# A message product in three rounded products, every second message unsplit, in the edge stage of a graph network kernel

## What is computed

```python
h = jnp.maximum(_layernorm(x, axis=-1), 0.0)
m_in = jnp.concatenate([h[src], edge_attr], axis=1)      # 512 + 128 features
m = jax.nn.relu(m_in @ W1.T + b1) @ W2.T + b2
agg = jax.ops.segment_sum(m, dst, num_segments=h.shape[0])
```

## Time and profile before

| | us |
|---|---|
| median of 3 runs | 1405.14 (1401.69 to 1405.39) |
| the profiled execution | 1408.71 |
| its span, first to last instruction | 1407.0 |
| cell stage, 292 to 527 | 235 |
| P stage, 757 to 808 | 51 |
| edge stage, 808 to 1116 | 308 |
| TensorE / VectorE / GpSimd / ScalarE busy over the span | 1260.4 / 1015.7 / 713.9 / 582.9 |

### The profile page before, as it was taken

One profiled execution on the slowest core, in us unless ns is written; L12 is line 12 of the kernel. 1 busy time (PEld: TensorE's weight loads), 2 busy tenths in 40 slices (PEclk: granted clock), 3 DMA queues, 4 the chain that ended last, 5 costly groups with the idle time before them and its releaser, 6 DMA issues.

```text
span 1407.0 us, 20310 instructions
## 1 busy us (share of the span) xinstructions
PE 1260.4 (90%) x4504; PEld 753.1 (54%) x4504; DVE 1015.7 (72%) x1944; ACT 582.9 (41%) x1470; POOL 713.9 (51%) x873
## 2 busy tenths in 40 slices
PE   4764989949898889899997889999999899998998
PEld 2532444423333335457875644445445488886787
DVE  9568625359899889752368568889898799888543
ACT  0210221146666650212011178888888743334210
POOL 0577677767787761776667066666667300000000
PEclk9987999979999999999999999999999999999999
DMA  8851252230000008334224477777777300002231
GB/s 331 292 167 31 91 179 67 68 130 25 17 19 17 17 6 312 116 112 136 83 83 136 161 225 215 223 230 225 222 221 229 93 0 1 0 1 86 75 94 36
DMA packets 87257, 167.93 MB, mean 119 GB/s; under 512 B 16124, under 2 KB 44670, under 8 KB 84644
## 3 DMA queue, kind: packets, MB, share of 16 engines
q1 hardware_dynamic: 59588, 102.72, 22.0%
q0 software_dynamic: 25472, 59.97, 14.2%
q10 hardware_dynamic: 2144, 4.59, 1.1%
HBM read 115.97 MB, written 51.25 MB: 119 GB/s over the span
## 4 chain that ended last, share of the span: by engine, by line
PE 44%; issue 22%; POOL 15%; DVE 9%; DMA 6%; DVEq 2%; POOLq 1%; ACT 1%; SPq 0%; ACTq 0%
POOL cell_rows L707 9%; PE pb L1231 6%; PE pb L1239 6%; PE pb L1434 5%; POOL arena L818 5%; PE pb L1407 4%; PE pb L1408 4%; PE pb L1409 4%; DMA arena<-p_rows,gidx 4%; DVE arena L1690 2%; PE pb L1339 2%; PE pb L1205 2%; PE pb L1123 2%; DMA cell_rows<-tiles,gidx 2%; PE pb L1311 1%
## 5 line engine op out<-in xcount | busy, mean ns | idle before, releaser
L818 POOL DMA_INDIRECT arena<-p_rows,gidx x184 | 191.6, 1042 | 65.4 <-issue 64.5
L753 POOL DMA_INDIRECT dst_rows<-ering,gidx x168 | 168.6, 1004 | 103.1 <-issue 95.7
L707 POOL DMA_INDIRECT cell_rows<-tiles,gidx x168 | 169.1, 1007 | 68.0 <-issue 53.8
L1339 PE MATMUL pb<-arena 128*128 128x512 f32 x368 | 189.8, 599 | 4.3 <-ACT arena L990 4.3
L1690 DVE TENSOR_TENSOR arena<-pb,arena 128x384 f32 x272 | 151.8, 558 | 26.6 <-PE pb L1205 24.4
L1827 DVE TENSOR_TENSOR arena<-pb,arena 128x512 f32<-128x512 f32 x184 | 124.2, 686 | 39.9 <-DMA arena<-p_rows,gidx 29.7
L881 ACT ACTIVATE arena<-iota,free 128x128 f32<-128x128 f32 x272 | 94.3, 393 | 86.3 <-PE pb L1205 69.7
L1205 PE MATMUL pb<-arena 128*128 128x384 f32 x272 | 105.6, 515 | 19.1 <-POOL arena L760 19.1
L1205 PE MATMUL pb<-tiles,arena 128*128 128x384 f32 x272 | 103.3, 505 | 19.7 <-DVE arena L1690 17.0
L1355 PE MATMUL pb<-high,low 128*128 128x512 f32 x138 | 92.0, 666 | 8.2 <-DVE arena L1842 5.4
L1834 DVE SCALAR_TENSOR_TENSOR low<-arena,high 128x512 fp32r<-128x512 f32 x138 | 94.5, 685 | 3.4 <-issue 0.8
(11 more groups left out here) (307 smaller groups left out, 2539.6 us busy)
## 6 DMA issues: line engine op xcount, KB each, us to landing
dst_rows<-arena SPq DMA_DIRECT2D x6, 2046.0 KB, 17.5
ering<-in_edge_attr_dram SPq DMA_DIRECT2D x41, 256.0 KB
arena<-adj SPq DMA_DIRECT2D x10, 640.0 KB, 4.1
arena<-dst_rows SPq DMA_DIRECT2D x24, 264.0 KB
arena<-wt_gru SPq DMA_DIRECT2D x48, 128.0 KB
ws<-dst_rows SPq DMA_DIRECT2D x22, 264.0 KB
arena<-in_x_dram SPq DMA_DIRECT2D x18, 256.0 KB
arena<-in_L_gnn_W_hh_dram SPq DMA_DIRECT2D x3, 1024.0 KB
```

Source lines behind the costliest of these rows:

```text
L707: nc.gpsimd.indirect_dma_start(cell_rows[:, :], bass.IndirectOffsetOnAxis(gidx[:, SPAN * a + k:SPAN * a + k + 1], 0), cring[:, a, k], None ...
L753: nc.gpsimd.indirect_dma_start(dst_rows[:, :], bass.IndirectOffsetOnAxis(gidx[:, k:k + 1], 0), ering[:, k, :], None).then_inc(e_scattered[ ...
L818: nc.gpsimd.indirect_dma_start(rows[:, k, :], None, p_rows[:, :], bass.IndirectOffsetOnAxis(gidx[:, k:k + 1], 0)).then_inc(g_landed[k], 16)
L1339: nc.tensor.matmul(e_bank(k)[:], erowT[:, k % 4], w1e_sb, start=True, stop=True).then_inc(edge_mm, 1)
```

## The change

In the **edge stage** the attributes are split too. ScalarE copies them rounded (`erowT[:, 0]`), a new VectorE operation `low_row` subtracts that from the bank and writes the rest (`erowT[:, 1]`), and `m_edges` is three rounded products with W1e split in the same way (`w1e_high`, `w1e_low`, made once). Since VectorE now reads the bank as well, `t_edges` and `m_edges` wait for a new semaphore `row_split`, which `low_row` raises. TensorE and ScalarE turn and copy attributes five chunks ahead in place of four; `low_row` runs four ahead. Every second message is summed whole (`SPLIT = 0`), in place of every fourth. GpSimd reads the sources' numbers where they lie in the loaded columns, with no copy to `gidx`; SP's loads therefore wait for `msg_added`, where they waited for `g_ready`.

In the **P stage** tiles 0 and 1 are turned one step of the second layer earlier, and `low_h2` of tiles 0 to 2 is made within that layer. The reciprocal and the products of the batch norm are made behind the last tile of P; the variance is loaded later, to another place. In the **cell stage** VectorE loads 32 addresses at a time (`READ`), in 9 turns for 17.

```diff
-WHOLE = 3
+SPLIT = 0
...
+        erowT = sb_behind(low.shape[1] + 6 * KT * D + GROUP * (D + EW), "erowT", [P, 2, 4, P], F32R)
...
+        READ = 4 * TURN
...
-                    at_least(sp, g_ready, WIDE // 4 * i + q - 3)
+                    at_least(sp, msg_added, WIDE * i + 4 * q - 12)
...
-            def index_quarter(i, q):
...
-                nc.gpsimd.tensor_copy(gidx[:, k:k + 4], edge_rows(4 * q, 4).bitcast(I32)[:, :, DE]).then_inc(g_ready, 1)
...
+                    nc.gpsimd.indirect_dma_start(rows[:, k % GROUP, :], None, p_rows[:, :],
+                                                 bass.IndirectOffsetOnAxis(edge_rows(k).bitcast(I32)[:, 0, DE:DE + 1], 0)
+                                                 ).then_inc(g_landed[k % GROUP], 16)
...
-                nc.scalar.copy(erowT[:, k % 4], pb[k % 2][:, 0:P]).then_inc(turned_read, 1)
+                nc.scalar.copy(erowT[:, 0, k % 4], pb[k % 2][:, 0:P]).then_inc(turned_read, 1)
...
-                    if not last or k + 4 < n:
-                        turned_copy(c + 4, k + 4)
+                    if not last or k + 5 < n:
+                        turned_copy(c + 5, k + 5)
...
-                at_least(pe, turned_read, c - 1)
+                at_least(pe, row_split, c - 1)
                 nc.tensor.transpose(pb[k % 2][:, 0:P], edge_rows(k)[:, 0, 0:DE], ident[:]).then_inc(turned, 1)
...
-                pe.wait_ge(turned_read, c + 1)
+                pe.wait_ge(row_split, c + 1)
                 at_least(pe, msg_added, c - 3)
-                nc.tensor.matmul(e_bank(k)[:], erowT[:, k % 4], w1e_sb, start=True, stop=True).then_inc(edge_mm, 1)
+                nc.tensor.matmul(e_bank(k)[:], erowT[:, 0, k % 4], w1e_high[:], start=True, stop=False)
+                nc.tensor.matmul(e_bank(k)[:], erowT[:, 0, k % 4], w1e_low[:], start=False, stop=False)
+                nc.tensor.matmul(e_bank(k)[:], erowT[:, 1, k % 4], w1e_high[:], start=False, stop=True).then_inc(edge_mm, 1)
...
-                if t == NT - 1:
-                    pe.wait_ge(h_ready, NT + 1)
-                    turn_tile(("h2T", 0), h[:, 0])
+                if t == NT - 2:
+                    for k in range(2):
+                        pe.wait_ge(h_ready, NT + k + 1)
+                        turn_tile(("h2T", k), h[:, k])
...
-                    inverse_root("bn", var_v, vts(var_v, var_v, BN_EPS, None, ALU.add))
-                    link(vtt(sc_v, sc_v, var_v, ALU.mult))
...
+            dve.wait_ge(root_ready, ROOT["bn"] + 1)
+            link(nc.vector.reciprocal(var_v, var_v))
...
+            def low_row(i, k):
+                dve.wait_ge(turned_read, WIDE * i + k + 1)
+                vtt(erowT[:, 1, k % 4], pb[k % 2][:, 0:P], erowT[:, 0, k % 4].bitcast(F32), ALU.subtract).then_inc(row_split, 1)
...
                 for k in range(n):
+                    if not last or k + 4 < n:
+                        low_row(i + (k + 4) // WIDE, (k + 4) % WIDE)
                     if not last or k + 2 < n:
                         message(i + (k + 2) // WIDE, (k + 2) % WIDE)
```

More of the change, by code:

```diff
@@ L1856, in _ @@
             turns = DST_CHUNKS // WIDE
+            dve.wait_ge(w1e_split, 1)
+            for k in range(4):
+                low_row(0, k)
             message(0, 0)
```

135 lines of the change are left out of this document (68 added, 67 removed).

## The result

The changed kernel takes 1423.38 us in the median of 4 runs (1419.88 to 1428.35), the kernel before 1405.27 us beside it (4 runs, 1401.69 to 1408.51). The ratio is 1.0129, 95% interval 1.0099 to 1.0158: slower by 18 us. The forecast was 1425.5, slower by 20.4, with a range of its own of 1409 to 1441 and a chance of 0.77 for slower. The profiled spans are 1423.9 and 1407.0 us, 16.9 apart.

| | before | after | change | forecast |
|---|---|---|---|---|
| start to first addition of the cell stage | 300.4 | 299.7 | -0.7 | 0 |
| first to last addition of the cell stage | 227.2 | 225.8 | -1.4 | -3.4 |
| from there to the squares of tile 9, second layer | 240.2 | 238.8 | -1.4 | 0 |
| from there to the first `message` | 47.1 | 41.1 | -6.0 | -9 |
| first to last `message` | 297.0 | 324.8 | +27.8 | +33 |

A forecast was written before the change was run, and what follows sets the result against it. TensorE's work was taken to bound most of the edge stage, GpSimd's chain costing 0.09 us a chunk more. Edge +33, P -9 and cell -3.4 make +20.6 on a median of 1405.14: 1425.5 us, range 1398 to 1442.

The forecast's parts named there:

- The ring: Edge stage: turning, copy, relu, `low`, `add_sums`, `low_row`, next turning wait in a circle, 3.57 us per two chunks, 1.785 a chunk.
- The signs that it named for the ring: Edge stage: `message` 3.5 to 3.7 us a pair, `low` 0.03 behind relu, TensorE idle some 0.4, GpSimd off the chain.
- The two that it named for the other stages: P stage: first message near 803 us; cell stage: loads of 32 addresses of about 1.95 us.
- rival A: Edge stage: ring doesn't close, engines' work sets 1.49 us a chunk; 1368 us in all, chance 0.14.
- The edge stage: First to last message: 183 distances at 1.785 plus 3 us make 330 us for 297, +33 us, ends +4 and +51.
- the P stage: Tiles drawn forward, reciprocal behind the last tile: first message moves from 814.9 to 806, -9 us, between -3 and -12.
- the cell stage: VectorE's address loads, 9 for 17 with the same number of addresses: -3.4 us, between 0 and 10 saved.
- rival A's 5 us for the four-pass arithmetic: Edge stage, within rival A: three rounded products at 3/4 of a plain one would make TensorE some 5 us less.
- rival D: P stage: drawn tiles bring nothing, since VectorE's reciprocal behind the last tile gives all back; 1432 us with the ring, chance 0.08.
- The 3 us for loop ends: Edge stage: 3 us added for eleven loop ends, where TensorE was seen to stand for a branch.
- The engines alone: Edge stage by each engine's own work: TensorE 1.45, VectorE 1.485, ScalarE 1.39 us a chunk; stage at about 1.49.
- the prediction's bound of 0: Cell stage: lower end of the loads' gain, 0 us if an address costs more in a long load.

The follow-up runs named there:

- (3): Changed kernel with one more ScalarE copy of 128 x 128 a pair, behind the copy of an even chunk's turned attributes: 1440.84 us, ratio 1.0255.
- (4): Changed kernel with one more VectorE copy of 128 x 128 a pair, right ahead of `low`'s wait: 1425.38 us, ratio 1.0150.
- (1): Changed kernel with VectorE's `low_row` moved behind `message`, ahead of `low`, and one chunk further ahead: 1375.72 us, ratio 0.9797.
- the open kernel: The kernel of (1): changed kernel with `low_row` ahead of `low` and one chunk further ahead; 1375.72 us, pace 1.509 us a chunk.
- experiment 7: Two kernels against the open kernel: one more VectorE copy a pair ahead of `low`, 1378.55 us; one of three rounded products left out, 1367.22 us.
- (9): The open kernel with batch norm's reciprocal back in the middle of the P stage, 1372.98 us; in two halves with a third store buffer, 1372.14 us.

## Why the prediction was right

**The ring, step by step.** It was forecast from rows of a kernel that had no ring. Beside the forecast what the trace after shows: turning to copy 0.32 + 0.05, measured 0.37 (937.11 to 937.48); copy to relu 0.87, measured 0.87 (to 938.35); relu to `low` 0.66, measured 0.65 (to 939.00); `low` to `add_sums` 0.73, measured 0.73; to `low_row` 0.60, measured 0.61 (940.34); `low_row` and the hop 0.28 + 0.06, measured 0.33. Sum 3.57 forecast, 3.56 measured. The signs that it named for the ring hold: 3.56 us a pair, `low` 0.03 behind the relu, TensorE idle for 0.40 ahead of every other turning, GpSimd off the chain. The two that it named for the other stages don't quite: the first message came at 805.4, not near 803, and loads of 32 take 2.10, not 1.95. That it is this ring and not the engines' work (rival A) is shown, not argued: a cost inside it is paid in full (3), the same kind of cost beside it is free (4), and the ring opened without an instruction less gives 48 us (1).

**The total was closer than its parts.** The edge stage was put 5.2 us too high, the P stage and the cell stage 3.0 and 2.0 too low, and that they cancel is luck. On the spans the change is 16.9 us for 20.6, and the rest of that is the 3.5 us of the three rows forecast at 0. The recorded sums have small slips of their own: 1405.14 + 20.6 is 1425.7, not 1425.5; rival A's 5 us for the four-pass arithmetic are 0.035 x 183 = 6.4; and rival D's 1432 has 3 us of gain in the P stage, though it is said to bring nothing (that would be 1434.7).

**The edge stage, +27.8 for +33.** The 3 us for loop ends were not far off: within the loop a round takes 3.55 to 3.58 us, but three of each eight (one turn of the loop, 16 chunks) take 3.59 to 3.68, so that eight take 28.73, 0.2 more than 8 x 3.565, about 2 us over ten turns. What was left out are the ends of the stage: the first eight rounds, ahead of the loop, take 3.45 on average, and the last two, where nothing is turned any more, 2.80 and 2.59. That is 2.7 us less; the rest is ends of half a round and the 0.01 us of the round.

**The engines alone.** TensorE's 1.45 stands at 1.465 in the open kernel, and the three rounded products at 0.23 apart cost 0.69, where 0.68 was taken from a run of thirty equal ones. VectorE's 1.485 was too high: I took `low_row`'s recorded 0.28 us as its cost on the engine, where the step to the next start is 0.20; it is 1.40. The forecast didn't hang on it, but my later expectation of experiment 7 did and missed by 11 us or more.

**The P stage, -6.0 for -9.** On the clock of before the last addition ends at 799.2, forecast 797.5; the tail to the first `low_row` takes 6.3 us, forecast 6.0; and from there to the message 3.4, forecast 2.4. The rows, answering:

```profile
795.02 0.69 DVE L1807 TENSOR_TENSOR tiles<-pb,arena 128x512 f32<-128x512 f32 x1 [0.77 <-DMA p_rows<-tiles]
795.74 3.35 DVE L1819 RECIPROCAL tiles<-tiles 128x512 f32<-128x512 f32 x1
...
801.98 0.49 DVE L1829 TENSOR_TENSOR erowT<-pb,erowT 128x128 fp32r<-128x128 f32 x2 [0.24 <-DVE vec L1823]
803.20 0.50 DVE L1829 TENSOR_TENSOR erowT<-pb,erowT 128x128 fp32r<-128x128 f32 x2 [0.73 <-ACT erowT L984]
805.40 0.69 DVE L1835 TENSOR_TENSOR arena<-pb,arena 128x512 f32<-128x512 f32 x1 [1.70 <-PE pb L1335]
```

Two things were left out. The last addition waits 0.77 us for the store that empties its buffer, where I had counted TensorE's tiles alone (their last product ends at 794.16, 797.7 on the clock of before, for 797). And TensorE, idle for 6.2 us in the tail, starts the edge stage at half its clock: the granted clock is the third column from the end, 0.50 from 801 to 806 us, so 1.2 of 2.4 GHz.

```profile
801.00:806.00 5.00, 3.02 (x8) 2.29 (x9) 2.29 (x7) 1.02 (x4) 3.78 (x5) 0.50 0.77 233
```

Rounded products then follow each other in 0.43 us, for 0.23 in the steady stage:

```profile
804.73 0.63 PE L1335 MATMUL pb<-w1e_high,erowT 128*128 128x512 f32 x1
805.16 0.63 PE L1333 MATMUL pb<-w1e_high,erowT 128*128 128x512 f32 x1
```

Three of them stand ahead of the first message, 0.6 us. (The kernel before has such a stretch too, but behind its first message: 0.79 from 818 to 823 us.) Rival D, that the tail takes all back, is wrong in the sum, but half of its reason holds: the reciprocal's move brings nothing (9). The distance from the squares of tile 9 is 41.6 us with the tiles drawn and the reciprocal left in the middle, 47.1 before, and 46.3 before with the indices in place, so it is the drawn tiles that bring nearly all of the 6.0 us.

**The cell stage, -1.4 for -3.4.** I took 0.053 us an address for all lengths; from 16 to 32 addresses it is (2.102 - 1.098) / 16 = 0.063, so a load of 32 takes 2.10 and not 1.95. VectorE stands 2.29 to 2.35 us at each of them in the loop, in place of twice 1.285. That an address costs more in a long load was what the prediction's bound of 0 stood for, and the truth lies nearer to that bound. The Trainium skill ("DMA: Bandwidth & Descriptors", Latency and other measured facts) gives a floor of about 600 ns for a `tensor_load`; the trace disagrees for loads of one address: the 92 of the changed kernel's edge stage take 299 to 328 ns, 304 in the median.

## What to carry to other kernels

Before a step is given to another engine, write down what stands in front of it in that engine's queue: here 0.28 us of work that frees a bank stood behind a wait for a third engine, and that closed a ring over three engines which costs more than the work saved. Sum such a ring from the starts of like operations, and compare it with each engine's own need. If it is longer, first try to move the freeing step ahead of the wait, which cost nothing here; more buffers may only send the ring through the next thing behind the same wait. Once no ring is left, the gain of a cheaper product is at most the distance to the next engine: here TensorE needs 1.465 us a chunk, VectorE 1.40 and ScalarE 1.39, and 0.23 us taken off TensorE brought 0.033, since VectorE's need and rows that land late stood behind it.

## What the runs showed of the hardware

- VectorE follows an operation of 128 columns (recorded 0.28 us) with the next after 0.20 us, and one from SBUF to SBUF of the same size (0.21) after 0.13; recorded durations are 0.07 to 0.08 too long as costs in a busy queue.
- A table load of 32 addresses takes 2.10 us, of 16 1.10, of one 0.304 to 0.306 in the median: an address costs a little more in the longer load.
- Three rounded products of 512 columns cost 0.69 us between starts (0.23 each) at the clock's upper level and 1.29 (0.43 each) at the lower one, in this loop.
- The stores of P, 256 KB each, take 2.0 us from issue to landing in the median, but one kept VectorE waiting until 780.55 in the changed kernel, 9.7 us behind the end of the addition at 770.14 that filled its buffer. Loads of 256 KB that took 8.3 and 9.7 us to land ran in the same stretch; that they held the store up was not tested.
